# DLRM tower with a CIN stack: the top layers in four sets of 64 samples, and other pair sizes

## The reference

```python
xk = x0                                    # [512, 32, 16]
for W in (W0, W1, W2):                     # [32, 32 or 64, 64]
    xk = relu(einsum('bmd,bhd,mhk->bkd', x0, xk, W))
    outs.append(sum(xk, axis=2))           # [512, 64]
h = concatenate([outs[0], outs[1], outs[2], dense_ctx], axis=1)   # 208
h = maximum(h @ W_top1 + b_top1, 0)        # 512
h = maximum(h @ W_top2 + b_top2, 0)        # 256
y = h @ W_top3                             # 1
```

## Time and profile before

| | |
|---|---|
| median of 3 runs | 353.35 us (351.65 to 353.98) |
| the profiled execution | 353.74 us |
| its span, first to last instruction | 351.9 us |
| TensorE, matmul busy | 305.4 us (87%) |
| VectorE busy | 274.2 us (78%) |
| GpSimd busy | 254.2 us (72%) |
| ScalarE busy | 61.6 us (18%) |
| mean granted TensorE clock | 0.985 of full |

### The profile page before, as it was taken

One profiled execution on the slowest core, in us unless ns is written; L12 is line 12 of the kernel. 1 busy time (PEld: TensorE's weight loads), 2 busy tenths in 40 slices (PEclk: granted clock), 3 DMA queues, 4 the chain that ended last, 5 costly groups with the idle time before them and its releaser, 6 DMA issues. The chain is left out here.

```text
span 351.9 us, 3914 instructions
## 1 busy us (share of the span) xinstructions
PE 305.4 (87%) x1476; PEld 112.7 (32%) x1476; DVE 274.2 (78%) x173; ACT 61.6 (18%) x122; POOL 254.2 (72%) x193
## 2 busy tenths in 40 slices
PE   0016859798999988999999999999999999998986
PEld 0013513243334222323333333233333334333426
DVE  0024949799999969999999999999999788954201
ACT  1001210301220330012201220222031104113011
POOL 5775678879788988888898879898919567917000
PEclk9999996999999999999999999999999999999998
DMA  5374956957973984286338643952580102100000
GB/s 178 45 251 83 369 111 180 376 88 213 381 149 65 279 329 80 28 337 260 56 71 303 272 72 77 378 190 61 151 327 0 45 2 63 45 2 0 0 0 0
DMA packets 52282, 52.07 MB, mean 148 GB/s; under 512 B 37574, under 2 KB 42568, under 8 KB 49064
## 3 DMA queue, kind: packets, MB, share of 16 engines
q1 hardware_dynamic: 41272, 39.92, 34.2%
q10 hardware_dynamic: 6896, 10.85, 11.5%
q0 software_dynamic: 4096, 1.06, 3.0%
HBM read 41.33 MB, written 2.10 MB: 123 GB/s over the span
## 5 line engine op out<-in xcount | busy, mean ns | idle before, releaser
L519 DVE TENSOR_TENSOR z_vector<-left,r_forms 128x2048 f32<-128x2048 f32 (+3 forms) x140 | 260.0, 1924 | 45.4 <-DMA r_forms<-x_rows 23.0
L569 PE MATMUL result<-z_vector,w_sb 128*64 128x512 f32 (+2 forms) x1056 | 213.9, 557 | 41.5 <-DVE z_vector L519 40.2
L309 POOL DMA_INDIRECT gathered_rows<-table,row_index x128 | 121.8, 951 | 41.2 <-issue 34.5
L324 POOL TENSOR_TENSOR z_pool<-r_forms,xj_forms 128x1024 f32<-128x1024 f32 (+2 forms) x60 | 131.8, 2232 | 24.7 <-PE result L569 15.0
L569 PEld LDWEIGHTS result<-z_vector,w_sb 128*64 128x64 f32 x1056 | 77.3, 142 | 172.9 <-issue 143.4
L569 PE MATMUL result<-z_pool,w_sb 128*64 128x512 f32 (+2 forms) x240 | 51.8, 571 | 0.0
L384 ACT ACTIVATE x_sb<-result 128x512 f32<-128x512 f32 (+2 forms) x27 | 14.9, 551 | 169.7 <-PE result L569 169.7
L499 DVE TENSOR_REDUCE d_sums<-x_sb 128x32 f32<-128x512 f32 (+2 forms) x27 | 16.8, 625 | 20.0 <-ACT x_sb L384 20.0
L569 PEld LDWEIGHTS result<-z_pool,w_sb 128*64 128x64 f32 x240 | 15.7, 136 | 34.1 <-issue 33.2
L368 ACT ACTIVATE left<-xj_forms 128x512 f32<-128x512 f32 (+2 forms) x36 | 18.6, 547 | 17.1 <-DMA xj_forms<-x_sb 6.8
L359 ACT ACTIVATE left<-h_form 128x512 f32<-128x512 f32 (+2 forms) x18 | 10.0, 553 | 59.8 <-DVE z_vector L519 44.9
(11 more groups left out here) (32 smaller groups left out, 28.1 us busy)
## 6 DMA issues: line engine op xcount, KB each, us to landing
r_forms<-x_rows SPq DMA_DIRECT2D x24, 1024.0 KB, 10.4
r_forms<-x_rows SPq DMA_DIRECT2D x8, 768.0 KB, 6.8
xj_forms<-x_sb ACTq DMA_DIRECT2D x24, 256.0 KB, 4.0
h_form<-x_rows SPq DMA_DIRECT2D x12, 256.0 KB, 3.0
gathered_rows<-table,row_index POOLq DMA_INDIRECT x128, 3.3
r_forms<-x_rows SPq DMA_DIRECT2D x4, 512.0 KB, 6.1
x_rows<-gathered_rows SPq DMA_DIRECT2D x24, 64.0 KB, 2.5
xj_forms<-x_sb ACTq DMA_DIRECT2D x8, 192.0 KB, 3.1
```

The lines of the kernel that those rows point to most:

```text
L309: nc.gpsimd.indirect_dma_start(gathered_rows[:, half % GATHERED, g], None, table, bass.IndirectOffsetOnAxis(ap=row_index[:, at:at + 1], ax ...
L324: nc.gpsimd.tensor_tensor(z_pool[:, unit % NZP, t, :, 0:columns(p)], r_form(q, p, t)[:, s0:s1], xj1_forms[form_buffer(n, p)][:, t, 0:colum ...
L519: nc.vector.tensor_tensor(z_vector[:, unit % NV, t, 0:s1 - s0, 0:columns(p)], left[:, t, bank, 0:columns(p)].unsqueeze(1).broadcast_to([12 ...
L569: done = nc.tensor.matmul(result[n][K * t:K * t + K, 0:columns(p)], weights, z[:, t, 0:columns(p)], start=first, stop=last)
```

## The change

The tiles get other sizes: 16, 16 and seven times 32 samples. The top layers run in four sets of 64 samples of each half (128 columns), with tiles of their own (`top_in`, `hidden1`, `hidden2`, `y_sb`) and one PSUM bank for the three layers. Set 0 (the pairs 0 to 2) and set 1 (pairs 3 and 4) are worked on in the loop over the pairs, at p = 4, 5 and p = 6, 7; set 2 (pairs 5 and 6) with layer 2 of the pairs 7 and 8. The last set (pairs 7 and 8) has the first half of its first layer ahead of the last unit of layer 2 of pair 8. To make room, the base of the tables is added in place, and the scratch for GpSimd's gather descriptors goes from 8192 to 4096 bytes of a partition. ScalarE issues the transfers of `y`. The number of chunks that GpSimd takes in each stage stays as it is.

```diff
-SAMPLES = [16, 24] + [32] * 6 + [24]
+SAMPLES = [16, 16] + [32] * 7
...
-EARLY = NP - 2
-EARLY_COLUMNS, LATE = 2 * START[EARLY], 2 * (START[NP] - START[EARLY])
+GROUP_ENDS = [3, 5, 7, 9]
+TOP1_AT = [4, 6]
+GS = B // 8
+GC = 2 * GS
...
+        top_in = sb("top_in", [128, 2, 2, GS])
+        hidden1 = sb("hidden1", [128, N1, GC])
+        hidden2 = sb("hidden2", [128, N2, GC])
+        y_sb = sb("y_sb", [1, GC])
...
+            def top_out(group, y):
+                if group > 0:
+                    act.wait_ge(y_stored, 16 * group)
+                nc.scalar.activation(y_sb[:], y, ACT.Copy).then_inc(y_ready, 1)
+                act.wait_ge(y_ready, group + 1)
+                act.dma_start(out.rearrange("(t b) o -> o t b", t=2)[:, :, samples(group)],
+                              y_sb[:].rearrange("o (t b) -> o t b", t=2)).then_inc(y_stored, 16)
...
+                if p in TOP1_AT:
+                    group = TOP1_AT.index(p)
+                    load_dense(group)
+                    top_inputs(group, range(3))
+                    top_hidden1(group)
+                if p - 1 in TOP1_AT:
+                    group = TOP1_AT.index(p - 1)
+                    act.wait_ge(top3_summed, group + 1)
+                    top_out(group, top3_psum)
...
-            act.wait_ge(z_vector_ready, 2 * vector_after((2, EARLY - 1)))
-            act.wait_ge(z_pool_ready, 2 * pool_after((2, EARLY - 1)))
-            act.dma_start(top_in[K:K + D, 1], dense).then_inc(top_loaded, 16)
-            early_inputs()
+            third, fourth = 2, 3
+            load_dense(third)
+            top_inputs(third, range(3))
...
+            def top1(group):
+
+                for k in range(N1):
                     for half, rows in enumerate((128, K + D)):
...
+                        done = nc.tensor.matmul(top1_psum[k], w_top1_sb[0:rows, half, 128 * k:128 * k + 128],
+                                                top_in[0:rows, half], start=half == 0, stop=half == 1)
+                done.then_inc(top1_summed, 1)
...
+                layer(1, p, {1: ([lambda: select(2, p - 1)] if p > 0 else [])
+                             + ([lambda: top2(TOP1_AT.index(p - 1))] if ended else [])})
                 vector_unit(0, p + 1, 0)
                 squares(p + 1)
+                if ended:
+                    top3(TOP1_AT.index(p - 1))
                 if p > 0:
-                    layer(2, p - 1, {1: [lambda: select(1, p + 1)]})
+                    layer(2, p - 1, {1: [lambda: select(1, p + 1)],
+                                     "pool": [lambda: whole_top1(TOP1_AT.index(p))] if made else []})
...
             layer(1, last, {1: [lambda: select(2, last - 1)]})
-            early(0)
-            layer(2, last - 1, {0: [lambda: early(1)], 1: [lambda: select(2, last), lambda: early(2)],
-                                "pool": [lambda: early(3)]})
-            layer(2, last, {0: [lambda: early(N1)], 1: [lambda: early(N1 + 1)], "pool": [lambda: early(N1 + N2)]})
...
+            whole_top1(2)
+            layer(2, last - 1, {1: [lambda: select(2, last), lambda: top2(2)]})
+            layer(2, last, {0: [lambda: top3(2)], "pool": [late_top1_begun]})
...
-    nc = bacc.Bacc("TRN2", target_bir_lowering=False, num_devices=1, dynamic_dma_scratch_size=8192)
+    nc = bacc.Bacc("TRN2", target_bir_lowering=False, num_devices=1, dynamic_dma_scratch_size=4096)
```

More of the change, by code:

```diff
@@ L290, in _ @@
                     load_r1(p, t)
[L292 to L296, removed]
+            sp.wait_ge(y_stored, 16 * len(GROUP_ENDS))
         @block.gpsimd
@@ L398, in load_xj1 @@
                                   ).then_inc(xj1_loaded[buffer][t], 16)
[L400 to L409, removed]
@@ L411, in early_inputs @@
-            def early_inputs():
-                for n in range(3):
-                    act.wait_ge(x_summed[n], EARLY)
-                    for t in range(2):
[L415 to L427, removed]
@@ new lines, in top_hidden2 @@
+            def top_hidden2(group):
+                act.wait_ge(top2_summed, group + 1)
+                for m in range(N2):
+                    nc.scalar.activation(hidden2[:, m], top2_psum[m], ACT.Relu,
+                                         bias=b_top2_sb[:, m:m + 1]).then_inc(hidden2_ready, 1)
+            def top_out(group, y):
+                if group > 0:
+                    act.wait_ge(y_stored, 16 * group)
[3 more added lines that the diff above has]
+                              y_sb[:].rearrange("o (t b) -> o t b", t=2)).then_inc(y_stored, 16)
@@ new lines, in top1, with late_top1 @@
+            def top1(group):
+                for k in range(N1):
+                    for half, rows in enumerate((128, K + D)):
+                        done = nc.tensor.matmul(top1_psum[k], w_top1_sb[0:rows, half, 128 * k:128 * k + 128],
+                                                top_in[0:rows, half], start=half == 0, stop=half == 1)
+                done.then_inc(top1_summed, 1)
+            def late_top1(half):
+                rows = (128, K + D)[half]
+                for k in range(N1):
+                    done = nc.tensor.matmul(late1_psum[k], w_top1_sb[0:rows, half, 128 * k:128 * k + 128],
+                                            top_in[0:rows, half], start=half == 0 and k % 2 == 0,
+                                            stop=half == 1 and k % 2 == 1)
+                    if half == 1 and k % 2 == 1:
+                        done.then_inc(late1_summed, 1)
@@ new lines, in whole_top1, with top2 @@
+            def whole_top1(group):
+                pe.wait_ge(top_loaded, 16 * 6)
+                pe.wait_ge(dense_loaded, 16 * (group + 1))
+                pe.wait_ge(top_in_ready, 6 * (group + 1))
+                if group > 0:
+                    pe.wait_ge(y_ready, group)
+                top1(group)
+            def top2(group):
+                pe.wait_ge(hidden1_ready, N1 * (group + 1))
+                for m in range(N2):
+                    for k in range(N1):
+                        done = nc.tensor.matmul(top2_psum[m], w_top2_sb[:, k, 128 * m:128 * m + 128], hidden1[:, k],
+                                                start=k == 0, stop=k == N1 - 1)
+                done.then_inc(top2_summed, 1)
@@ new lines, in top3, with late_top1_begun @@
+            def top3(group):
+                pe.wait_ge(hidden2_ready, N2 * (group + 1))
+                for m in range(N2):
+                    done = nc.tensor.matmul(top3_psum, w_top3_sb[:, m:m + 1], hidden2[:, m],
+                                            start=m == 0, stop=m == N2 - 1)
+                done.then_inc(top3_summed, 1)
+            def late_top1_begun():
+                pe.wait_ge(top_in_ready, 6 * (len(GROUP_ENDS) - 1) + 4)
+                pe.wait_ge(y_ready, len(GROUP_ENDS) - 1)
+                pe.wait_ge(x_ready[0], NP)
+                late_top1(0)
```

135 lines of the change are left out of this document (56 added, 79 removed).

## The result

| | before | after |
|---|---|---|
| median, on the same chip | 352.58 us (4 runs, 351.65 to 353.98) | 363.12 us (4 runs, 359.21 to 364.25) |
| the profiled execution | 353.74 us | 363.96 us |
| its span | 351.9 us | 362.1 us |
| mean granted TensorE clock | 0.985 | 0.971 |

The ratio of the times is 1.0276, with a 95% interval of 1.0186 to 1.0366. The changed kernel is slower, and the interval leaves open whether by more or less than 2%. The forecast was 364.4 us, 3.1% more.

The account below looks back on a forecast made before the run. TensorE was taken as nearly the bound in the middle and alone the bound over the last 126 us. The terms summed to +11.0 us on 353.74, 364.7, or 364.4 against the median; range 357.5 to 370.5.

Parts of the forecast that it names:

- the early set goes: Top layers' early set of 400-column matmuls leaves TensorE's path: -13.35 us.
- three sets of 64: Sets 0 to 2 add small 128-column matmuls on TensorE, 5.3 us a set: +15.9 us.
- pair 8: Last pair grows from 24 to 32 samples, wholly in the stretch that TensorE sets: +8.3 us.
- late half moved into the middle: Half of the last set's first layer moves into layer 2 of pair 8, still TensorE's time: +1.3 us.
- hidden slack and the late ReLU: TensorE's idle time in the middle hides 1.2 us of set 0; pair 7's layer 2 ReLU no longer late, -0.5.
- the end: After the last sum: halved first layer -1.1 us, wider last ReLU and sum 0.11 + 0.13, second layer +0.4.
- the front: Smaller pair 1 gives back 1.3 us at best, TensorE's slow restart at pair 2 costs 2.3: +1.0 us together.
- the rule weighed in the prediction: Weight loads of 107 ns overlap only in another row group: 0.40 us a matmul at 112 columns; not used in the sum.
- Small matmuls at the low clock's price: Rival: in the sets, 0.43 us per 128-column matmul, 7.4 us a set, 371 us in all; chance 8%.
- No slow restart: Rival: TensorE's pause before pair 2 is shorter or its rate back at once, -1.3 for +1.0, 362.1 us; 18%.
- The front is won: Rival: pair 1's 8.9 us of VectorE work are kept, wait near 64 us stays at 2.3, 354.5 us; 8%.
- Slower gathers: Rival: halved descriptor scratch slows GpSimd's gathers, 5.5 us more a pair at two in flight, over 380 us; 4%.

Follow-up runs that it names:

- the sets only: The changed kernel with the old pair sizes (16, 24, six of 32, 24), so only the four sets are new: 352.3 us, ratio 0.9987 to the kernel before.
- doubling a layer: The changed kernel with the first top layer of sets 0, 1 and 2 computed twice: 366.6 us, ratio 1.0413 to the kernel before.
- the experiment with the sizes alone: The kernel before with only the new pair sizes (16, 16, seven of 32), its early and late set kept: 363.4 us, ratio 1.0311.
- the three other kernels of the first series with 16 samples in pair 1: New sizes alone on the kernel before, 363.4 us; changed kernel with ten spare matmuls ahead of pair 2, 358.6; changed kernel with the sets' first layer twice, 366.6.
- the second series: Later runs on another chip, with the changed kernel repeated unchanged: 367.0 us against 364.2 for the kernel before, ratio 1.0084.

## Why the prediction was right

By its own terms, in us:

| term | predicted | measured | from |
|---|---|---|---|
| the early set goes | -13.35 | -13.35 | no such row in the chain after |
| three sets of 64 | +15.9 | +13.2 | what is left of TensorE's 9.21 more; the rows, 3 x (1.98 + 1.98 + 0.53), say 13.5 |
| pair 8 | +8.3 | +8.3 | TensorE busy in the middle, 192.95 against 184.64 with the sets only |
| late half moved into the middle | +1.3 | +1.09 | 0.64 + 0.45 |
| hidden slack and the late ReLU | -1.7 | -1.33 | TensorE's idle time, 2.15 to 0.82 |
| the end | -0.46 | -0.47 | 9.96 to 9.49 |
| the front | +1.0 | +2.8 | mark, 156.05 to 158.84 |
| sum | +11.0 | +10.2 | spans, 351.9 to 362.1 |

**What it rested on held.** TensorE sets the pace behind the front, and what is put there is paid in full: doubling a layer gave 5.37 for 5.37. The arithmetic that pair 8's columns are the same in number and not in place is the loss, by the experiment with the sizes alone.

**Three sizes were off, and that the sum came within 0.8 us is in part luck.** The sets were priced 2.7 us too high, the front 1.8 too low, and the hidden slack 0.4 too high. The sets cost 4.4 to 4.5 us each and not 5.3. I scaled the late set's row of 0.28 us for 112 columns; in dense work a small matmul takes 0.25 for 128 columns, and added to one of its kind 0.22. The row of 112 columns stood behind a pause in the end, not in dense work. By the rate of the 400-column rows (0.72 us), streaming 128 columns is 0.23, so the weight load hardly shows in dense work, where I had priced it in. The 0.21 that the prediction gives for streaming only comes from no row, and three sets at 0.43 a matmul are 22.2 us, not 23; neither went into the sum. By the rule weighed in the prediction (the Trainium skill, "TensorE: Matmul & The Clock Gate", sections LDWEIGHTS and The mechanism) an estimate for 128 columns is 0.21 + 0.21 = 0.43 us (0.44 with the 0.23 of the rows for streaming). The rows of the sets, 1.98 us for eight, disagree with it.

And the front cost 2.8 in place of 1.0. The wait of 7.62 us was forecast (about 8), and the slow start also (1.9 measured, 2.3 taken). The 1.3 given back came too: from the end of pair 2's first unit to the mark are 83.35 us before (72.70 to 156.05), 82.18 after, and 81.78 to 82.07 in the three other kernels of the first series with 16 samples in pair 1, so 1.2 to 1.6 less (84.02 with the sets only, where pair 1 has 24). What the sum had no term for is the start of that unit, 71.10 against 69.05 before, 2.05 us late: 2.05 + 1.91 - 1.17 = 2.79. In those three other executions it was 0.0, 0.1 and 0.8 late, so this part is of the size of the scatter.

The agreement at the end (-0.46 and -0.47) is luck in its parts. I had -1.1 for the halved first layer and +0.4 for the second layer. They came as -0.67 (2.24 to 0.71 + 0.86) and -0.21 (3.23 to 3.02), and the second layer alone scattered from 2.10 to 3.66 us between executions of the kernels with sets.

**The chain turned earlier than said.** I put the change from VectorE to TensorE at about 185 us, where set 0 stands. The chain after is TensorE from 158.84 on. Once TensorE has no wait of its own at 190 and 225, the chain runs back through it to its last wait, the one of 0.74 at 158.84. The term for the slack came out near: I took 0.6 twice, by steps, and the waits that went were 0.41 twice; the late ReLU gave 0.52 for 0.5. One sign that I had named did not show: VectorE was to idle more from 200 to 330 us, and it idled 16.5 us there against 17.5 before. What idles less is TensorE, 0.00 against 1.72 us.

**The rivals.** Small matmuls at the low clock's price: refuted, 0.25 against 0.43 us. No slow restart: refuted by the four slow starts. The front is won: VectorE's wait was 7.62 us and not 2.3, so refuted. Slower gathers: refuted by 1.25 us each, and GpSimd's products of two successive pairs begin 33.88 us apart (147.66 and 181.54 in its timeline), where it was 33.94. What I had not thought of is that the front of the kernel before can itself be 10 us longer, and then the same change costs under 1% (1.0084 in the second series).

## What to carry to other kernels

Work that is equal in sum isn't equal in time: samples taken from a pair in the front, where a transfer comes last, and given to the last pair, where one engine never waits, cost their full price (8.3 us for eight) and gave back 1.2 to 1.6 us. Cut the span at an event that all versions have. Here the 180 to 200 us from the mark to the last ReLU repeated to 0.01 us in every series, while the part ahead scattered by more than the effect in question. When an engine runs behind another by tenths of a microsecond in a pair, look at its own idle rows, not at its share, for what may still be added.

## What the runs showed of the hardware

- The same kernel on the same chip took 352.7 us in one series and 364.1 in another. By their profiles the difference lies ahead of 166 us, and the longest wait in it is one of ScalarE, 13.07 us up to 57.25. With the gathers brought forward such a wait lasted 24.77 and 26.85 us; in the first of these ScalarE waited for a semaphore of TensorE's, whose matmuls had by their row ended 18.65 us before. The share of the DMA engines was 0.07 from 50 to 57 us of the first of these waits.
- After a pause of 3.6 us, TensorE's next four steps took 5.35 us instead of 3.65, after 7.78 they took 5.25, and after some 10.2 us 5.56 to 6.26. After 2.25 they ran at the full rate.
- The last second layer, 8 matmuls of 128 columns, had several prices at the same place in the program: 2.10 in seven executions of five kernels, 3.02 in the kernel after (granted clock of its end 0.80) and 3.66 in its second execution, 3.53 and 3.42 with GpSimd's early waits left out. That moves the end from 7.8 or 8.1 us to as much as 9.6, and I found no cause in the edits.
